# Holding half of a group's gathers on GpSimd until a matrix product has left TensorE

## The reference, cut to what matters

```python
x = x + gnn0(layernorm(x), adj)       # first stage
x = x + ffn0(layernorm(x))            # attention; 2 of 8 experts for a token
x = x + gnn1(layernorm(x), adj)       # last stage, with
x = x + ffn1(layernorm(x))            # 2 of 6 experts for a token

def gnn1(x, adj, weight, bias):
    d = (sum(adj, -1) + 1e-05) ** -0.5
    return (d[:, None] * adj * d[None, :]) @ (x @ weight) + bias
```

## Time and profile before

| | us |
|---|---|
| median of 3 runs (lowest to highest) | 863.1 (862.56 to 863.46) |
| the profiled execution, first to last instruction | 932.6 |
| of it the last stage, from the first `aT` of the steps | about 330 |

### The profile page before, as it was taken

The page is one execution under the profiler, slowest core; times in us unless marked ns, Lnnn a source line. Parts: engine busy times, 40 slices in busy tenths (PEclk is TensorE's granted clock), DMA queues, the critical chain, the costliest instruction groups (busy, mean ns, idle before and its releaser), DMA issues.

```text
span 932.6 us, 21565 instructions
## 1 busy us (share of the span) xinstructions
PE 846.5 (91%) x6286; PEld 649.8 (70%) x6287; DVE 698.3 (75%) x2699; ACT 515.8 (55%) x1072; POOL 433.0 (46%) x410
## 2 busy tenths in 40 slices
PE   7988898989866499999999998999998999999998
PEld 6656676766643399999999998755665555555564
DVE  5898777767743499887777786988887778777763
ACT  3666666756532355665666554456555555545554
POOL 3258777668744630092010022366665556656400
PEclk9999989989977799999999999999999999999999
DMA  9504211131000376666666674144333333433322
GB/s 252 158 24 106 67 41 41 44 99 41 31 23 26 109 205 181 174 181 182 172 172 161 168 182 114 43 141 151 118 115 114 107 107 122 135 112 132 121 80 90
DMA packets 104712, 108.25 MB, mean 116 GB/s; under 512 B 27279, under 2 KB 88673, under 8 KB 102465
## 3 DMA queue, kind: packets, MB, share of 16 engines
q1 hardware_dynamic: 94096, 88.52, 33.3%
q0 software_dynamic: 8880, 18.19, 6.5%
q10 hardware_dynamic: 1664, 0.66, 0.3%
HBM read 82.07 MB, written 25.26 MB: 115 GB/s over the span
## 4 chain that ended last, share of the span: by engine, by line
PE 52%; issue 6%; DVE 3%; POOL 2%; another core or an unknown queue 1%; ACT 1%; DVEq 0%; POOLq 0%; ACTq 0%
PE banks L2041 15%; PE banks L2081 10%; PE banks L2207 7%; PE banks L2199 6%; PE banks L2175 5%; PE banks L2056 2%; PE banks L2113 2%; POOL expert_rows L1336 1%; PE banks L2102 1%; PE banks L2221 1%; PE banks L2130 1%; PE banks L2151 1%; PE banks L2122 1%; PE banks L2142 1%
## 5 line engine op out<-in xcount | busy, mean ns | idle before, releaser
L1336 POOL DMA_INDIRECT expert_rows<-slots_out,slot_c x128 | 143.8, 1124 | 80.9 <-DVE ys L1580 45.0
L329 POOL DMA_INDIRECT slots_in<-flat,slot_now x120 | 123.3, 1027 | 46.8 <-issue 34.6
L2041 PE MATMUL banks<-xT_hi,w_hi 128*128 128x256 f32 (+1 forms) x426 | 126.1, 296 | 0.7 <-issue 0.4
L2041 PE MATMUL banks<-xT_hi,w_lo 128*128 128x256 f32 (+1 forms) x426 | 120.1, 282 | 0.0
L2041 PE MATMUL banks<-xT_lo,w_hi 128*128 128x256 f32 (+1 forms) x426 | 119.8, 281 | 0.0
L2081 PE MATMUL banks<-w_sb,prod 128*128 (+1 forms) x852 | 106.7, 274 | 0.0
L2081 PEld LDWEIGHTS banks<-w_sb,prod 128*128 128x128 f32 (+1 forms) x852 | 101.0, 191 | 0.5 <-issue 0.2
L2041 PEld LDWEIGHTS banks<-xT_hi,w_hi 128*128 128x128 f32 (+1 forms) x426 | 75.6, 177 | 1.4 <-issue 1.4
L2041 PEld LDWEIGHTS banks<-xT_lo,w_hi 128*128 128x128 f32 (+1 forms) x426 | 75.8, 178 | 0.0
L2041 PEld LDWEIGHTS banks<-xT_hi,w_lo 128*128 128x128 f32 (+1 forms) x426 | 75.6, 177 | 0.0
L1401 ACT ACTIVATE w_hi<-w_raw 128x684 fp32r<-128x684 f32 x71 | 54.9, 773 | 29.1 <-PE banks L2041 24.5
(11 more groups left out here) (303 smaller groups left out, 2187.9 us busy)
## 6 DMA issues: line engine op xcount, KB each, us to landing
f_all<-gates_dram SPq DMA_DIRECT2D x16, 1536.0 KB
w_raw<-in_w SPq DMA_DIRECT2D x71, 342.0 KB
xs<-slots_in SPq DMA_DIRECT2D x71, 128.0 KB
slots_out<-ys SPq DMA_DIRECT2D x71, 128.0 KB
base_all<-in_x SPq DMA_DIRECT2D x16, 256.0 KB, 4.2
out<-ob SPq DMA_DIRECT2D x16, 256.0 KB
slots_in<-zrow SPq DMA_DIRECT2D x20, 128.0 KB
adjt<-in_adj_t SPq DMA_DIRECT2D x32, 64.0 KB
```

The lines of the kernel that those rows point to most:

```text
L329: G.indirect_dma_start(out=slots_in, out_offset=bass.IndirectOffsetOnAxis(ap=slot_now0[g % 2][:, n:n + 1], axis=0), in_=flat[g % 2][:, n / ...
L1336: G.indirect_dma_start(out=rows[p][:, n, :], out_offset=None, in_=slots_out[0:filled(g) * R, :], in_offset=bass.IndirectOffsetOnAxis(ap=sl ...
L2041: last = T.matmul(banks[bank][0:m, half * R:(half + 1) * R], ww[:, par, n * HIDP + c * P:n * HIDP + c * P + m], xx[:, par, :], start=q == ...
```

## The change

GpSimd gets one more one-element addition between gather 3 and gather 4 of a group. It waits until `aT` of the group before has signalled, so gathers 4, 5, 6 and (in the next step) 7 are issued after that. `later(g[1], 2)` leaves it out for the first two groups; it acts in 13 steps that have gathers behind it (groups 3 to 15). The wait on `passed` keeps order between the additions themselves.

```diff
+            spare3 = sb("spare_e", [P, 1])
-            at = signals(sem, "pick held add0 ...
+            at = signals(sem, "pick held passed add0 ...
+                    def behind_aT(g):
+
+                        if g is not None:
+                            pool.wait_ge(at["aT"], g + 1)
+                            if has(g - 3):
+                                pool.wait_ge(at["passed"], g - 2)
+                            G.tensor_tensor(spare3[:, :], mhalf[:, 0:1], mhalf[:, 0:1], ALU.add).then_inc(at["passed"], 1)
+
                             gt(2, g[0], p[0])
                             rstd0(g[1])
                             gt(3, g[0], p[0])
+                            behind_aT(later(g[1], 2))
                             gt(4, g[0], p[0])
                             gt(5, g[0], p[0])
                             gt(6, g[0], p[0])
```

More of the change, by code:

```diff
@@ L1084, in build @@
             gateS = [sb(f"gateS{i}", [P, GT], f32r) for i in range(2)]
-            spare, spare2 = sb("spare_c", [P, 1]), sb("spare_d", [P, 8])
+            spare, spare2, spare3 = sb("spare_c", [P, 1]), sb("spare_d", [P, 8]), sb("spare_e", [P, 1])
             ld_w, ld_adj = sem("ld_w1"), [sem(f"ld_adj_c{i}") for i in range(2)]
@@ L1100, in build @@
             EVEN = DEEP + DEEP % 2
-            at = signals(sem, "pick held add0 add1 st0 mv0 var0 rstd0 scale xn xb aT tT gnn x3 "
+            at = signals(sem, "pick held passed add0 add1 st0 mv0 var0 rstd0 scale xn xb aT tT gnn x3 "
                               "st1 mv1 var1 rstd1 f3 f3T hi lo rh rhr logits "
```

## The result

| | us |
|---|---|
| before, median of 4 runs | 863.28 (862.56 to 868.34) |
| after, median of 4 runs | 880.96 (879.9 to 884.2) |
| ratio, 95% interval | 1.0205 (1.0171 to 1.0239) |
| after, the profiled execution, first to last instruction | 878.1 |

The change makes the kernel 17.7 us slower; 941 was forecast, 78 us slower. The direction and the range (865 to 963) hold, the size does not: per step it is 17.7 / 13 = 1.36 us, not 6.0. This time the profiled execution (878.1 us) fits its runs.

A forecast was written before the change was run, and what follows sets the result against it. It took the last stage to be bound by TensorE; to 863.1 us it added 13 groups x 5.0 us of waiting (65) and 13 x 1.0 us of lower clock (13), giving 941 us, range 865 to 963.

The forecast's parts named there:

- What bounds the stage: Last stage: TensorE bounds it, and whatever makes TensorE wait once in a group is paid in every group.
- Steps 1 and 2: GpSimd: first held gather starts 0.80 us after the release; the train of four takes 4.97 us.
- Step 3: Held gathers beside DVE's multiplications: 0.4 us added to the train, bounds 0 and 0.8.
- `f_all` ... comes 5.7 us after the release in every group: SP's load: nothing ahead of it is touched, so the last gather comes beside its start, 0.2 us behind.
- A gather that arrives after `f_all` waits until `f_all` is through: DMA queues: gather 7 lands near 671.4, `add0` starts 5.9 us later, TensorE waits 5.0 us a group; chance 0.50.
- slips in behind one packet: Rival, DMA queues: last gather waits for only part of `f_all`, transpose 1.3 us late a group, 880 us; chance 0.08.
- The price of a lost race: TensorE, each of 13 groups: 5.0 us of waiting (65 us) and 1.0 us for the lower clock (13 us).
- The 2.0 us: TensorE's clock after a wait: the most a group can lose more, from one group taking 23.5 instead of 21.5 us.
- that case: Gather 7 waits for `f_all` in nearly all groups: 941 us, bounds 924 to 962; chance 0.50.
- The won race: Rival: last packets go ahead of `f_all`, `add0` 1.05 us late, 0.45 us a group, 869 us; chance 0.12.
- mixed case: Rival: some groups win and some lose, half of 78 and half of 6 us, 905 us; chance 0.12.
- the way that the prediction left open: DMA queues: all of an engine's share of `f_all` may be one packet, after which the engine changes queues.

The follow-up runs named there:

- the earlier trace: Profile of the kernel before the change, which the prediction read; its span of 932.6 us was 69.5 us above the 863.1 of the runs.
- the addition alone: The changed kernel, but the added addition waits for the graph product of one group earlier, so no gather is held: 862.77 us.
- three held: The changed kernel with the addition moved behind gather 4, so three gathers are held instead of four: 862.60 us.
- five held: The changed kernel with the addition moved ahead of gather 3, so five gathers are held instead of four: 963.79 us.
- the later release: The changed kernel, four gathers held, but until ACT has copied the graph product out (`tT`) instead of until the product (`aT`): 957.3 us.

## Why the prediction was right in direction and wrong in size

**What bounds the stage:** right. TensorE, without a gap in 13 groups, and a wait in front of `f3T` is paid in full.

**Steps 1 and 2,** 0.80 us to the first gather and 4.97 for four: right, 0.77 to 0.88 in most groups and 5.01 (667.61 to 672.62). The 0.80 is the gather's own time to be ready, not the addition's, since a second addition fits into it. In three of the four groups that lose, the start is late (1.04 to 1.37); what delays it there is not settled.

**Step 3,** 0.4 us for the gathers beside DVE's multiplications: wrong. The 52 held gathers of the change take 1.01 to 1.08 us each; the 1.40 of the earlier trace rows was a single gather, not the rule.

**"`f_all` ... comes 5.7 us after the release in every group": this is the step that failed,** together with step 3. The forecast put the end of the last issue at 6.17 and `f_all` at 5.71, 0.46 behind. In nine groups the issue ends at 5.8 to 5.9, and `f_all` is issued at 6.16 to 6.31. The change touches none of the instructions ahead of `f_all`, as the prediction said, but one of them is a store of the gates through the same DMA engines. From its issue to that of `f_all` it takes 1.42 to 1.53 us where no gather is held (the profile with the addition alone); 1.71 to 2.05 in the nine groups, where the packets of the third held gather (5.27 to 5.74 us behind the release in the group of 666.74) and of the store (5.51 to 5.74) fall together; 1.43 to 1.59 in the four others. The store and the load with the addition alone; then the DMA queues from 671.88 to 672.25 and from 672.25 to 672.48 (group of 666.74), and from 752.89 to 753.21 (group of 747.76; q1 is SP's queue, the store is 12 packets):

```profile
667.23 0.29 SPq L1239 DMA_DIRECT2D gates_dram<-gateT  x1
668.66 0.34 SPq L1246 DMA_DIRECT2D f_all<-gates_dram  x1
...
q0 software_dynamic: 17, 0.07, 61.2%
...
q1 hardware_dynamic: 11, 0.01, 14.9%
q0 software_dynamic: 15, 0.00, 3.7%
...
q1 hardware_dynamic: 12, 0.01, 14.8%
```

In the four others the trains run differently: in the group of 747.76 the store's packets (5.14 to 5.45) pass between those of the second gather (4.46 to 4.96) and the third (5.76 to 6.24). So the train holds up the transfer that it races, and wins; where it starts too late to meet the store, `f_all` is in time, and it loses. What decides is the distance from the train's first gather to the store's issue: 3.45 to 3.67 us in the nine that win, 3.00 to 3.38 in the four that lose, also in that of 625.47, whose train is as early (0.87) as in some that win. That is also why no group lies in the middle of the table.

The packets' times say the same in all 91 groups of the seven runs that hold gathers and leave `f_all` free. In 56 of them a held gather's packets begin 0.78 to 0.97 us behind the store's issue, the store's own only 1.03 to 1.23 behind it, and it is 1.71 to 2.10 us to `f_all`'s issue (12 of these groups are of the run with three held, which has no fourth gather). In the other 35 no gather's packets begin in that stretch, the store's begin at 0.76 to 0.77, and it is 1.42 to 1.60 us, nearly as with the addition alone. No run moved the store by itself; that the gather's packets delay it rests on these times.

Each of the two errors is of a few tenths of a us, and that was enough. By an estimate from the table, without step 3's 0.4 us the forecast's sum ends the last issue at 5.77, 0.06 behind `f_all`, where a group loses 1.2 to 1.7 us and not 6: some 19 us over 13 groups. The delayed store then takes nine groups over to the side that wins.

**"A gather that arrives after `f_all` waits until `f_all` is through":** right from 0.59 us on, shown by the runs with five held and with the later release, and by what became of them when `f_all` was put behind. Nearer than that it is a matter of degree: at the forecast's own 0.46 the table says some 4.4 us, not the 5.7 of the sum, and at 0.05 to 0.15 the "slips in behind one packet" rival gives about the right loss (1.3 forecast, 1.2 and 1.7 measured), though not its way: the gather's packets begin ahead of `f_all`'s there and take longer.

**The price of a lost race:** the wait was 5.0 forecast, 4.75 in the one group that lost wholly, 5.4 with five held. The clock was 1.0 forecast and came to 1.5 in that group (21.51 us against 20.0), and to about 2.4 where every group loses, for the slow stretch there goes on behind the first 3.9 us (0.50, then 0.76 for 3.9 more). The 2.0 us were read from a row in which 1.0 us at full clock lies between the idle stretch and the slow one. Lost throughout, four held gathers cost 957, inside the bounds of that case (924 to 962).

**The won race:** the rival had 0.45 us a group, and the nine cost 0.5 on the mean (4.8 / 9). `add0` comes 2.0 us later than with the addition alone (7.5 for 5.4 to 5.7 behind the release), not 1.05 as the rival had it. The gather needs 1.5 to 1.7 us from the end of its issue and not 1.3, and the group of the earlier trace rows, from which the rival counted, has its `add0` at 6.04, later than any group with the addition alone. `f3_` behind it uses up the slack of `f3T`. Three held end 1.3 us earlier and stay inside the slack.

What came is the prediction's mixed case, with nine groups won and four lost in part or whole: 4.8 + 13.2. It had been given half and half, whole losses, and a chance of 0.12.

**The rule on DMA queues.** In 3.3 us with 81 packets of `f_all` none of the gathers' went. The Trainium skill ("DMA: Bandwidth & Descriptors", "Queues, rings and completion order") has an engine change queues after a whole packet, of typically 9 to 17 descriptors. The records of `f_all` are of 12 KB (1.00 MB in 81), so its 1536 KB are 128 records, 8 for each of 16 engines. If a record is a descriptor, an engine's whole share is no more than one such packet: the way that the prediction left open, with which this agrees. No run here shows the engines one by one.

## What to carry to other kernels

When work is moved to run beside a large transfer, work out the distance to that transfer's start as a difference of two chains, and look for what the moved work shares with each of them, DMA engines included: here a train 0.63 us later cost 76 us more, and the moved gathers shifted both ends. Where the margin is smaller than the scatter of a start, don't bet on one side in all groups; put the order down with a wait (the load behind the gathers: 871 for 881, and 888 for 964), or move one transfer fewer (three held: free). And take the slack from the profile of a harmless variant when that of the kernel itself is stretched.

## What the runs showed of the hardware that was not expected

- A small store (12 KB) that meets the packets of an indirect gather starts 0.3 to 0.5 us later (1.03 to 1.23 us behind its issue for 0.76 to 0.77): 1.71 to 2.10 us to the issue that waits for it, in 56 groups of seven runs, for 1.42 to 1.53 where no gather is held.
- A gather queued behind a wait starts some 0.8 us after the release (0.77 to 0.90 in most groups), whether one or two additions of 0.2 to 0.4 us stand between.
- After 4.75 us without matmuls TensorE's granted clock was 0.60 for 3.9 us in the change, and after 1.95 us 0.57 for as long; in the run that waits in every group it was, after 4.76 us, 0.50 for 3.9 us and 0.76 for as long again.
